# A selective-scan stack on one core: decay factors in four SBUF buffers, a four-bank PSUM ring, and a new table of places

## The chip, the cores and the metric

The kernel runs on one core of one Trainium2 chip. The metric is the device time of one execution in microseconds (us). The engines are TensorE (PE in the rows), VectorE (DVE), ScalarE (ACT), GpSimd (POOL) and SyncE (SP), which issues the DMAs. PEld is TensorE's weight load.

## The reference

A layer norm of x (4 sequences of 1024 tokens, 256 wide) feeds two branches: eight selective-scan layers, and a routed feed-forward with eight experts. The result is x + s * silu(f). The diff touches the layers alone. One of them computes:

```python
xz = jnp.einsum('bld,ed->ble', x, Wi)
xin, z = jnp.split(xz, 2, axis=-1)
xin = _silu(_causal_conv(xin, cw, cb))
x_dbl = jnp.einsum('blc,ec->ble', xin, Wx)
delta = jax.nn.softplus(jnp.einsum('blr,cr->blc', dt_raw, Wdt) + bdt)
A = -jnp.exp(Alog)
# for each time step, with a state h of 512 channels x 16
h = h * jnp.exp(d_t[..., None] * A) + (d_t * u_t)[..., None] * B_t[:, None, :]
y = jnp.einsum('bcn,bn->bc', h, C_t)
# behind the scan
y = (y + u * Dp) * _silu(z)
x = x + jnp.einsum('blc,dc->bld', y, Wo)
```

## The kernel before

`program` runs `experts`, then `mamba`, then `finish`. Only `mamba` is changed.

**Units and tiles.** The work of `mamba` is cut into 64 units: 8 layers, 4 sequences, and 2 halves of 512 time steps. A unit has 16 steps, one for each state index n, and each step has 4 tiles, one for each block of 128 channels. A tile (n, j) has number k = 4n + j and is 128 channels by 512 time steps. A tile is made as follows:
- ScalarE computes the decay, exp(delta * A), in `exponent` (L907), into one of two PSUM buffers `ps_d`. It waits until the scan two tiles back has read the buffer.
- GpSimd multiplies du by the row of B, which a DMA has repeated over the partitions in `brep`, giving the drive (L875). There are eight drive buffers, so GpSimd may be eight tiles ahead of the scans.
- VectorE runs the recurrence as one scan instruction over 512 time steps in `scan` (L1069), into one of two state buffers for the step. In second halves (h = 1) it starts from `carry`, which GpSimd copies (L861) from the last column of the first half.

When a step's four scans are done, TensorE turns the state (`turn_state`, L1225; four transposes for each of four blocks of time), ScalarE multiplies by C while it copies out (`weigh`, L914, to `prod`), and TensorE turns the product back and adds it up in `ps_y` over the 16 steps (`turn_back`, L1232).

**The ring.** All other results of TensorE pass through the same ring `ps_r`, which has two banks, in a fixed order with the turned states: the count of overflows CNT, the two output projections O0 and O1 of the unit before, X0 to X3 and Z0 to Z3 (input projections), C3 (the convolution of one channel block, by matmul), XD (B, C and the time-step rank), BC (B and C turned) and DT0 to DT3. TensorE writes into a bank when what lay in it has been read (`place`, `place_free`). ScalarE reads most of the items, VectorE reads CNT, O0 and O1.

**Three units at a time.** In unit U the engines also do the early part of unit U+2 (marks, liveness, mask, X, convolution), the late part of U+1 (XD, delta, du, Z) and the end of U-1 (gates, output projection, residual add). Where each piece stands is given by tables: `RING_AT` for TensorE, and `SILU_AT`, `EXP_AT`, `LN_AT` for ScalarE, `MARK_AT`, `ALIVE_AT`, `ADD_AT`, `GATE_AT`, `SOFT_AT`, `CONV_AT`, `DU_AT` for VectorE, `HALO_AT`, `XM_AT` for GpSimd. A pair (n, j) means: behind tile j of step n. Each engine runs its list in order, and semaphores tie the lists together. ScalarE reads a ring item one place behind the one where TensorE makes it (`READ_AT`).

**The silus.** At `SILU_AT` ScalarE does the silu of xc (L942) and of z (L946), 2048 elements each, between two loads of function tables (L942, L1020).

**Marks and liveness.** VectorE marks values over a limit (L1078, L1080, to `over`), TensorE counts them, and a running minimum (L1091, to `alive`, one buffer for each half) gives a mask. GpSimd multiplies the input by it (L846, to `xm`), and a DMA stores its first row.

**Other names in the rows.** `xc` is the convolution, with a first tap (L1104) and further taps (L1108) on VectorE for three channel blocks; `low`, `soft`, `relu` and `delta` are the steps of softplus (L1127, L1130, L1134, L1137); `du` is delta * u (L1117); the gates are L1167 and the residual add is L1173.

Of the kernel before, what the change touches and what calls it, by code (L numbers as in the profile page):

```python
# [25 lines left out]
F32 = mybir.dt.float32  # L26
# [45 lines left out]
XD = RANK + 2 * STATES  # L72
BREP = 4
DRIVE = 8
CARRY_LAG = 9
TABLE = "natural_log_exp_and_others"


RING_AT = {"CNT": (3, 0), "O0": (4, 1), "O1": (5, 3), "XD": (4, 2), "BC": (7, 3), "DT0": (6, 0), "DT1": (6, 2), "DT2": (8, 0),
           "DT3": (9, 2), "Z0": (10, 1), "Z1": (11, 3), "Z2": (14, 1), "Z3": (15, 0), "X0": (5, 0), "X1": (8, 3),  # L80
           "X2": (10, 3), "X3": (14, 2), "C3": (17, 0)}
SILU_AT, EXP_AT, LN_AT = (4, 2), [(7, 0), (10, 1)], [(8, 3), (11, 3)]
MARK_AT, ALIVE_AT, ADD_AT = [(2, 1), (2, 2)], (3, 1), [(4, 3), (6, 1)]
PE_CONV, DVE_CONV = [3], [0, 1, 2]
GATE_AT, SKIPY_AT = [(1, 1), (1, 2), (1, 2), (1, 2)], [(1, 1), (1, 3), (1, 3), (1, 3)]
SOFT_AT = [(7, 3), (8, 3), (9, 3), (10, 2), (10, 3), (11, 3), (14, 2), (14, 3)]
CONV_AT = [(5, 2), (5, 2), (6, 0), (6, 2), (9, 2), (10, 1), (12, 2), (12, 3), (15, 1), (17, 0), (17, 3), (19, 0)]
DU_AT = [(14, 3), (14, 3)]
HALO_AT, XM_AT = (3, 2), (5, 1)
CONV_ITEMS = [f"C{j}" for j in PE_CONV]  # L90
CV = CB - len(PE_CONV)
READ_AT = {name: divmod(CB * n + t + 1, CB) for name, (n, t) in RING_AT.items()}
# [509 lines left out]
def item_place(U, h, kind, name):  # L602

    i = ITEMS[kind].index(name)
    if isinstance(items_before(U, kind)[0], int):
        return (items_before(U, kind)[0] + i) % 2
    return (h * len(ITEMS["mid"]) + PRE_ALL + i) % 2


def item_ready(U, kind, name):  # L610
# [22 lines left out]

def place_free(U, kind, name):

    i = ITEMS[kind].index(name)
    if kind == "pre0" and i < 2:
        return None
    act, vec = reads(U, kind, i - 1)
    if i >= 2 and ITEMS[kind][i - 2] in VEC_ITEMS:  # L640
        return "vec", vec
    return "act", act


def mamba(nc, w_in, w_x, w_dt, w_out, w_skip, w_conv, a_log, par, xres, ident, alive_dram, bc_dram, rate_dram):

    with ExitStack() as ctx:
# [13 lines left out]
        ones_time = sb("ones_time", [1, T], BF16)  # L661
        zeros = sb("zeros", [P, 1])

        over = sb("over_mark", [P, 2, DB, T], BF16)
        alive = [sb(f"alive{h}", [P, T]) for h in range(2)]
        xm = [sb(f"xm{h}", [P, DB, T]) for h in range(2)]
        low = sb("low", [P, 2, T])
        xpad = sb("xpad", [P, CB, TAPS - 1 + T])
# [12 lines left out]

        brep = sb("brep", [P, BREP, T])
        drive = sb("drive", [P, DRIVE, T])
        state = [sb(f"state{k}", [P, CB, T]) for k in range(2)]
        carry = sb("carry", [P, STATES, CB])
        prod = sb("prod", [P, TC, INNER])

        ps_d = ctx.enter_context(nc.psum_tensor("ps_d", [P, 2, T], F32))
        ps_r = ctx.enter_context(nc.psum_tensor("ps_r2", [P, 2, 512], F32))
        ps_y = ctx.enter_context(nc.psum_tensor("ps_y", [P, CB, T], F32))  # L690

        par_in, par_exp, par_set, par_out = sem("par_in"), sem("par_exp"), sem("par_set"), sem("par_out")
# [15 lines left out]
        def is_first(U):  # L708
            return isinstance(U, int) and U == 0
# [13 lines left out]
        def _(sp):  # L723
# [22 lines left out]
            def store_alive(U, kind, G):  # L746
                h = G % 2
                sp.wait_ge(ring_vec, item_read(U, kind, "CNT"))
                c = (G // HALVES % BATCH) * SEQ + h * T
                sp.dma_start(alive_dram[:, c:c + T], alive[h][0:1, :]).then_inc(alive_out[h], 16)  # L750

            def store_bc(U, kind, F):
                sp.wait_ge(ring_act, item_read(U, kind, "XD"))
# [81 lines left out]
        def _(pool):  # L835
# [5 lines left out]
            def mask_x(U, kind, G, h, it):  # L841
                pool.wait_ge(ring_vec, item_read(U, kind, "CNT"))
                if not (isinstance(G, int) and G < 2):

                    pool.wait_ge(ring_ready, items_before(U, kind)[0])
                nc.gpsimd.tensor_tensor(xm[h][:], xres[:, :, bass.ds((it % BATCH) * SEQ + h * T, T)],  # L846
                                        alive[h][:].unsqueeze(1).to_broadcast([P, DB, T]), ALU.mult).then_inc(xm_set, 1)

            def halo(U, kind, F, h):

# [45 lines left out]
        def _(act):  # L896
            def exponent(U, h, k):

                n, j = divmod(k, CB)
                if k in (0, CB // 2):  # L900
                    act.wait_ge(delta_set, 2 * U + k // 2 + 1)
                if not (is_first(U) and k < 2):
                    act.wait_ge(scanned, TILES * U + k - 1)
                a = j * STATES + n
                if k == 0:
                    act.wait_ge(cur_in[h], loads_of(U, h))
                nc.scalar.activation(ps_d[:, k % 2, :], delta[h][:, j, :], ACT.Exp, scale=cur[h][:, a:a + 1]).then_inc(decay_set, 1)  # L907
# [137 lines left out]
            exponent(0, 0, 0)  # L1045
            exponent(0, 0, 1)
# [5 lines left out]
        def _(dve):  # L1052
            def scan(U, h, it, kind, n, j):
                k = CB * n + j
                dve.wait_ge(decay_set, TILES * U + k + 1)
                dve.wait_ge(drive_set, TILES * U + k + 1)
                if j == 0 and not (is_first(U) and n < 2):

                    if n >= 2:
                        dve.wait_ge(ring_ready, item_ready(U, kind, ("S", n - 2, TC - 1)))  # L1060
                    elif n == 1:
                        dve.wait_ge(ring_ready, item_ready(U, kind, ("S", "prev", TC - 1)))
                    else:
                        dve.wait_ge(ring_ready, items_before(U, kind)[0])
                    if h == 0 and n >= 2:
                        dve.wait_ge(carried, STATES * it + n - 1)
                    if h == 1:
                        dve.wait_ge(carried, STATES * it + min(STATES - 1 + n, STATES))
                nc.vector.tensor_tensor_scan(state[n % 2][:, j, :], ps_d[:, k % 2, :], drive[:, k % DRIVE, :],  # L1069
                                             carry[:, n, j:j + 1] if h == 1 else 0.0, ALU.mult, ALU.add).then_inc(scanned, 1)  # L1070

            def mark_over(U, kind, F, h, it, side):

                if kind != "pre0":
                    dve.wait_ge(ring_vec, items_before(U, kind)[1])
                xs = xres[:, :, bass.ds((it % BATCH) * SEQ + h * T, T)]
                if side == 0:
                    nc.vector.tensor_scalar(over[:, 0], xs, LIMIT, None, ALU.is_gt).then_inc(over_set, 1)  # L1078
                else:
                    nc.vector.tensor_scalar(over[:, 1], xs, -LIMIT, None, ALU.is_lt).then_inc(over_set, 1)  # L1080

            def keep_alive(U, h, kind, F, hf):

                dve.wait_ge(ring_ready, item_ready(U, kind, "CNT"))
                if not (isinstance(F, int) and F < 2):
                    dve.wait_ge(xm_set, F - 1)
                    if isinstance(F, int):
# [444 lines left out]
```

## Time and profile before

| | |
|---|---|
| median of 3 runs | 7806.82 us (7770.17 to 7848.79) |
| profiled execution | 7796.76 us, span 7795.0 us |
| TensorE busy | 6935.7 us (89%), weight load 4781.3 us (61%) |
| VectorE busy | 6645.2 us (85%), 6512 instructions |
| ScalarE busy | 6436.9 us (83%) |
| GpSimd busy | 5919.1 us (76%) |
| DMA | 352.40 MB, 45 GB/s |

The profile is one execution. A group line gives the source line, the engine, what is written and read, the number of instructions, their busy time and mean, and the idle time of the engine in front of them with what ended it. A timeline row gives a start, a length and how many equal instructions are merged in it; it can start before the stretch asked for. The end of one instruction overlaps the start of the next on an engine by about 0.08 us. Ends of matmuls are modelled, so TensorE is better read from starts.

### The profile page before, as it was taken

Reading aid. Unit: us, or ns where it says so; the run is one execution under the profiler, and the core shown is the slowest. Engines: PE = TensorE matmul, PEld = TensorE weight load, DVE = VectorE, ACT = ScalarE, POOL = GpSimd, SP = SyncE. Lnnn points to the kernel's source line nnn. Section 1 sums busy time; section 2 is a strip of 40 time slices with the busy share of each in tenths; the row PEclk is TensorE's granted clock in tenths of the full one; section 3 lists DMA queues with packets and bytes.
Section 4 is the critical chain, followed back from the end, with each engine's and each line's share of the span. In section 5 each row is a group of like instructions: output and inputs, shape, how many; then the busy total and the mean of one; then the engine's idle time right before and its main releaser. Section 6 shows DMA issues by size and latency. Waiting matters only on the chain. (4 is left out here: it accounts for less than half of the span.)

```text
span 7795.0 us, 144019 instructions
## 1 busy us (share of the span) xinstructions
PE 6935.7 (89%) x39999; PEld 4781.3 (61%) x40063; DVE 6645.2 (85%) x6512; ACT 6436.9 (83%) x10314; POOL 5919.1 (76%) x4917
## 2 busy tenths in 40 slices
PE   6978999888999999999899999999998899999887
PEld 4646666666666666666666666666666666666665
DVE  3259888988988898889888988988898898889888
ACT  2248888888888888888888888888888888888887
POOL 2137888787888888888878887888888778888875
PEclk9989999999999999999999999999999999999998
DMA  4111111111111111111111111111111111111112
GB/s 160 33 40 37 39 40 47 42 38 38 42 45 43 39 39 43 46 40 40 39 46 44 40 38 42 45 42 39 39 47 42 38 39 42 45 43 39 39 38 90
DMA packets 222613, 352.40 MB, mean 45 GB/s; under 512 B 43856, under 2 KB 78448, under 8 KB 221712
## 3 DMA queue, kind: packets, MB, share of 16 engines
q1 hardware_dynamic: 218048, 332.70, 14.5%
q0 software_dynamic: 3792, 10.38, 0.4%
q8 instruction: 365, 5.98, 0.3%
q14 instruction: 408, 3.34, 0.1%
HBM read 325.00 MB, written 17.98 MB: 44 GB/s over the span
## 5 line engine op out<-in xcount | busy, mean ns | idle before, releaser
L875 POOL TENSOR_TENSOR drive<-du,brep 128x512 f32<-128x512 f32 x4096 | 5495.8, 1371 | 715.0 <-DVE du L1117 360.0
L907 ACT ACTIVATE ps_d<-delta,cur 128x512 f32<-128x512 f32 x4096 | 2844.6, 695 | 447.3 <-DVE state L1069 428.1
L914 ACT ACTIVATE prod<-ps_r,bcT 128x512 f32<-128x512 f32 x4096 | 2807.1, 685 | 240.0 <-PE ps_r L1225 235.4
L1225 PE MATMUL ps_r<-ident,state 128*128 128x128 f32 x16384 | 2552.5, 279 | 326.1 <-ACT prod L914 180.5
L1069 DVE TENSOR_TENSOR_SCAN state<-ps_d,carry,drive 128x512 f32<-128x512 f32 x2048 | 2503.2, 1264 | 308.9 <-PE ps_r L1225 274.8
L1069 DVE TENSOR_TENSOR_SCAN state<-ps_d,drive 128x512 f32<-128x512 f32 x2048 | 2390.7, 1207 | 300.8 <-PE ps_r L1225 239.6
L1232 PE MATMUL ps_y<-ident,prod 128*128 128x128 f32 x16384 | 2467.1, 275 | 25.9 <-ACT prod L914 25.9
L1232 PEld LDWEIGHTS ps_y<-ident,prod 128*128 128x128 f32 x16384 | 1928.7, 142 | 663.5 <-issue 511.7
L1225 PEld LDWEIGHTS ps_r<-ident,state 128*128 128x128 f32 x16384 | 1834.7, 141 | 773.4 <-ACT prod L914 497.3
L1273 PE MATMUL ps_r<-xm,w_inz_sb 128*128 128x512 f32 x1024 | 509.1, 620 | 89.3 <-ACT prod L914 89.3
L1265 PE MATMUL ps_r<-xm,w_inx_sb 128*128 128x512 f32 x1024 | 509.1, 621 | 25.4 <-ACT prod L914 13.9
L1313 PE MATMUL ps_r<-relu,w_out_sb 128*128 128x512 f32 x1024 | 474.2, 606 | 58.7 <-ACT prod L914 56.0
L1108 DVE SCALAR_TENSOR_TENSOR xc<-xpad,taps,xc 128x512 f32<-128x512 f32 x576 | 505.4, 877 | 4.2 <-issue 1.5
L861 POOL COPY carry<-state 128x4 f32<-128x4 f32 x512 | 226.3, 442 | 232.2 <-DVE state L1069 230.3
L1306 PE MATMUL ps_r<-xdbl,w_dt_sb 16*128 16x512 f32 x512 | 290.1, 647 | 90.2 <-DVE xres L1173 47.2
L1313 PEld LDWEIGHTS ps_r<-relu,w_out_sb 128*128 128x128 f32 x1024 | 184.7, 190 | 273.3 <-issue 217.7
L1273 PEld LDWEIGHTS ps_r<-xm,w_inz_sb 128*128 128x128 f32 x1024 | 174.4, 190 | 270.1 <-ACT prod L914 134.5
L1265 PEld LDWEIGHTS ps_r<-xm,w_inx_sb 128*128 128x128 f32 x1024 | 175.9, 191 | 196.0 <-issue 154.5
L534 ACT ACTIVATE hid<-ps_t,b_sb 128x128 f32<-128x128 f32 x312 | 84.8, 382 | 227.5 <-PE ps_t L495 227.5
L1292 PE MATMUL ps_r<-u,w_x_sb 128*48 128x512 f32 x512 | 233.7, 600 | 34.1 <-ACT u L942 34.1
L462 POOL DMA_INDIRECT ys_dram<-yb,row x39 | 37.4, 959 | 296.8 <-DVE yb L554 296.8
L1243 PE MATMUL ps_y<-u,skip 128*128 128x512 f32 x512 | 241.3, 594 | 4.6 <-DVE relu L1167 4.5
(148 smaller groups left out, 4586.5 us busy)
## 6 DMA issues: line engine op xcount, KB each, us to landing
brep<-bc_dram SPq DMA_DIRECT2D x1024, 256.0 KB, 3.2
w_sb<-w SPq DMA_DIRECT2D x8, 1024.0 KB
w_all<-w SPq DMA_DIRECT2D x8, 1024.0 KB, 11.4
xb<-xs_dram SPq DMA_DIRECT2D x39, 128.5 KB, 2.0
w_all<-x SPq DMA_DIRECT2D x4, 1024.0 KB, 9.0
w_inx_sb<-w_in SPq DMA_DIRECT2D x8, 512.0 KB, 4.0
w_inz_sb<-w_in SPq DMA_DIRECT2D x8, 512.0 KB, 4.4
w_out_sb<-w_out SPq DMA_DIRECT2D x8, 512.0 KB, 4.3
```

Of the source, the lines that this page charges most:

```text
L875: nc.gpsimd.tensor_tensor(drive[:, k % DRIVE, :], du[:, j, :], brep[:, n % BREP, :], ALU.mult).then_inc(drive_set, 1)
L907: nc.scalar.activation(ps_d[:, k % 2, :], delta[h][:, j, :], ACT.Exp, scale=cur[h][:, a:a + 1]).then_inc(decay_set, 1)
L914: nc.scalar.activation(prod[:, t, :], ps_r[:, item_place(U, h, kind, item), :], ACT.Copy, scale=bcT[(h + 1) % 2 if item[1] == "prev" else ...
L1069: nc.vector.tensor_tensor_scan(state[n % 2][:, j, :], ps_d[:, k % 2, :], drive[:, k % DRIVE, :], carry[:, n, j:j + 1] if h == 1 else 0.0, ...
L1108: step = nc.vector.scalar_tensor_tensor(xc[:, j, :], xpad[:, j, tap:tap + T], w, xc[:, j, :], ALU.mult, ALU.add)
L1225: last = nc.tensor.transpose(out[:, j * P:(j + 1) * P], state[n % 2][:, j, t * P:(t + 1) * P], ident[:])
L1232: last = nc.tensor.matmul(ps_y[:, j, t * P:(t + 1) * P], prod[:, t, j * P:(j + 1) * P], ident[:], start=False, stop=True, is_transpose=Tru ...
L1243: last = nc.tensor.matmul(ps_y[:, j, :], skip[:, j, :], u[:, j, :], start=True, stop=True, skip_group_check=True)
L1265: last = nc.tensor.matmul(out, w_inx_sb[:, k, j * P:(j + 1) * P], xm[h][:, k, :], start=(k == 0), stop=(k == DB - 1))
L1273: last = nc.tensor.matmul(out, w_inz_sb[:, k, j * P:(j + 1) * P], xm[hf][:, k, :], start=(k == 0), stop=(k == DB - 1))
L1306: nc.tensor.matmul(out, w_dt_sb[:, j * P:(j + 1) * P], xdbl[0:RANK, :], start=True, stop=True).then_inc(ring_ready, 1)
L1313: last = nc.tensor.matmul(out, w_out_sb[:, j, k * P:(k + 1) * P], gated[:, j, :], start=(j == 0), stop=(j == CB - 1))
```

## The change

- The decays go to four buffers `decay` in SBUF, no longer to two in PSUM. ScalarE starts four tiles ahead (`LEAD`), not two.
- The two banks that this frees go to the ring, which has four now (`RING`). `place_free` waits for the item four back, also over the border between units.
- SBUF is won for the decays: the marks lie in the second half of `soft`, and one `alive` buffer serves both halves. The marks wait until the delta of the next unit is made, and the liveness scan waits for the mask product and the DMA store of the half before.
- Every table of places is new. The silus stand at (2, 1), not at (4, 2). `LOW_AT` is added and used nowhere.

```diff
+LEAD = 4
+RING = 4
...
-SILU_AT, EXP_AT, LN_AT = (4, 2), [(7, 0), (10, 1)], [(8, 3), (11, 3)]
-MARK_AT, ALIVE_AT, ADD_AT = [(2, 1), (2, 2)], (3, 1), [(4, 3), (6, 1)]
+SILU_AT, EXP_AT, LN_AT = (2, 1), [(9, 1), (12, 3)], [(11, 2), (14, 0)]
+MARK_AT, ALIVE_AT, ADD_AT = [(1, 0), (1, 1)], (2, 2), [(2, 3), (4, 2)]
...
-HALO_AT, XM_AT = (3, 2), (5, 1)
+HALO_AT, XM_AT = (1, 3), (5, 1)
...
-    return (h * len(ITEMS["mid"]) + PRE_ALL + i) % 2
+    return (h * len(ITEMS["mid"]) + PRE_ALL + i) % RING
...
-    i = ITEMS[kind].index(name)
-    if kind == "pre0" and i < 2:
+    i = ITEMS[kind].index(name) - RING
+    if kind == "pre0" and i < 0:
         return None
-    act, vec = reads(U, kind, i - 1)
-    if i >= 2 and ITEMS[kind][i - 2] in VEC_ITEMS:
-        return "vec", vec
-    return "act", act
+    if i < 0:
+        before = {"pre1": "pre0", "first": "pre1", "mid": "mid", "near": "mid", "last": "near", "end": "last"}[kind]
+        assert not any(x in VEC_ITEMS for x in ITEMS[before][i:])
+        return "act", items_before(U, kind)[2] + i + 1
+    act, vec = reads(U, kind, i + 1)
+    return ("vec", vec) if ITEMS[kind][i] in VEC_ITEMS else ("act", act)
...
-        over = sb("over_mark", [P, 2, DB, T], BF16)
-        alive = [sb(f"alive{h}", [P, T]) for h in range(2)]
+        alive = sb("alive", [P, T])
...
+        over = soft[:, 2:4, :].rearrange("p a t -> p (a t)").bitcast(BF16).rearrange("p (s k t) -> p s k t", s=2, k=DB)
...
+        decay = sb("decay", [P, LEAD, T])
...
-        ps_d = ctx.enter_context(nc.psum_tensor("ps_d", [P, 2, T], F32))
-        ps_r = ctx.enter_context(nc.psum_tensor("ps_r2", [P, 2, 512], F32))
+        ps_r = ctx.enter_context(nc.psum_tensor("ps_r2", [P, RING, 512], F32))
...
-                if not (is_first(U) and k < 2):
-                    act.wait_ge(scanned, TILES * U + k - 1)
+                if not (is_first(U) and k < LEAD):
+                    act.wait_ge(scanned, TILES * U + k + 1 - LEAD)
...
-                nc.scalar.activation(ps_d[:, k % 2, :], delta[h][:, j, :], ACT.Exp, scale=cur[h][:, a:a + 1]).then_inc(decay_set, 1)
+                nc.scalar.activation(decay[:, k % LEAD, :], delta[h][:, j, :], ACT.Exp, scale=cur[h][:, a:a + 1]).then_inc(decay_set, 1)
...
-                        k = CB * n + t + 2
+                        k = CB * n + t + LEAD
...
-                nc.vector.tensor_tensor_scan(state[n % 2][:, j, :], ps_d[:, k % 2, :], drive[:, k % DRIVE, :],
+                nc.vector.tensor_tensor_scan(state[n % 2][:, j, :], decay[:, k % LEAD, :], drive[:, k % DRIVE, :],
...
                     dve.wait_ge(ring_vec, items_before(U, kind)[1])
+                    dve.wait_ge(delta_set, 2 if kind == "pre1" else 2 * U + 2)
...
-                if not (isinstance(F, int) and F < 2):
-                    dve.wait_ge(xm_set, F - 1)
+                if not is_first(F):
+                    dve.wait_ge(xm_set, F)
                     if isinstance(F, int):
-                        dve.wait_ge(alive_out[hf], 16 * (F // 2))
+                        dve.wait_ge(alive_out[1 - hf], 16 * ((F + hf) // 2))
```

VectorE's list from the start of unit 1, before. The gates are `relu<-ps_y,zs`, the marks `over_mark<-xres`, the residual add `xres<-xres,ps_r`; a scan is listed as SCALAR_TENSOR_TENSOR into `state`.

```order
L1069 SCALAR_TENSOR_TENSOR state<-ps_d,carry,drive 128x512
L1167 TENSOR_TENSOR relu<-ps_y,zs 128x512 x3
L1069 SCALAR_TENSOR_TENSOR state<-ps_d,carry,drive 128x512
L1108 SCALAR_TENSOR_TENSOR xc<-xpad,taps,xc 128x512
L1069 SCALAR_TENSOR_TENSOR state<-ps_d,carry,drive 128x512 x2
L1078 TENSOR_SCALAR over_mark<-xres 128x1024
L1069 SCALAR_TENSOR_TENSOR state<-ps_d,carry,drive 128x512
L1080 TENSOR_SCALAR over_mark<-xres 128x1024
L1069 SCALAR_TENSOR_TENSOR state<-ps_d,carry,drive 128x512 x2
L1108 SCALAR_TENSOR_TENSOR xc<-xpad,taps,xc 128x512
L1069 SCALAR_TENSOR_TENSOR state<-ps_d,carry,drive 128x512
L1091 SCALAR_TENSOR_TENSOR alive<-ps_r,alive,zeros 128x512
```

The same place of the changed kernel, from the first two gates on; the marks are `soft<-xres` now.

```order
L1173 TENSOR_TENSOR relu<-ps_y,zs 128x512 x2
L1114 SCALAR_TENSOR_TENSOR xc<-xpad,taps,xc 128x512
L1086 TENSOR_SCALAR soft<-xres 128x1024
L1074 SCALAR_TENSOR_TENSOR state<-decay,carry,drive 128x512
L1173 TENSOR_TENSOR relu<-ps_y,zs 128x512 x2
L1074 SCALAR_TENSOR_TENSOR state<-decay,carry,drive 128x512 x4
L1097 SCALAR_TENSOR_TENSOR alive<-ps_r,alive,zeros 128x512
L1074 SCALAR_TENSOR_TENSOR state<-decay,carry,drive 128x512
L1179 TENSOR_TENSOR xres<-xres,ps_r 128x512
```

Thirteen scans stood between the last gate and the first residual add (seven in the piece shown up to the liveness scan, six more behind it), and five stand there now. The marks come before the last gates, and the two conv taps that stood behind the gates have gone ahead.

ScalarE's list around the silus of unit 0, before.

```order
L914 ACTIVATE prod<-ps_r,bcT 128x512
L907 ACTIVATE ps_d<-delta,cur 128x512
L942 ACT_TABLE_LOAD
L942 ACTIVATE u<-xc 128x2048
L946 ACTIVATE zs<-zs 128x2048
L1020 ACT_TABLE_LOAD
L914 ACTIVATE prod<-ps_r,bcT 128x512
L907 ACTIVATE ps_d<-delta,cur 128x512
L954 ACTIVATE xdbl<-ps_r 48x512
```

The same in the changed kernel.

```order
L919 ACTIVATE prod<-ps_r,bcT 128x512
L912 ACTIVATE decay<-delta,cur 128x512
L947 ACT_TABLE_LOAD
L947 ACTIVATE u<-xc 128x2048
L951 ACTIVATE zs<-zs 128x2048
L1025 ACT_TABLE_LOAD
L919 ACTIVATE prod<-ps_r,bcT 128x512
L912 ACTIVATE decay<-delta,cur 128x512
```

Nine tiles (two steps and a tile) lie between the old place and the new. The decay in front of the table load is that of tile 20 before and of tile 13 now, and the copy of XD no longer stands right behind the silus.

## Rows read from the trace of the kernel before

**Rows 1.** Busy time by engine, 3000 to 4000 us; then TensorE's granted clock, DMA.
```profile
3000.00:4000.00 1000.00, 905.50 (x5320) 621.86 (x5328) 892.70 (x845) 875.12 (x1375) 810.83 (x661) 1.00 0.14 42
```
**Rows 2.** The scan's line: ns minimum/median/maximum, first and last start in us.
```profile
L1069 DVE TENSOR_TENSOR_SCAN state<-ps_d,drive x2048: 1189/1207/1226, 519.1 to 7640.6; 128x512 f32<-128x512 f32 x187
L1069 DVE TENSOR_TENSOR_SCAN state<-ps_d,carry,drive x2048: 1248/1259/1285, 632.0 to 7727.5; 128x512 f32<-128x512 f32 x187
```
**Rows 3.** VectorE's groups, 3000 to 4000 us: busy us, mean ns, idle before.
```profile
L1069 DVE TENSOR_TENSOR_SCAN state<-ps_d,drive 128x512 f32<-128x512 f32 x306 | 357.4, 1207 | 44.6 <-PE ps_r L1225 36.5 <-ACT ps_d L907 7.2
L1069 DVE TENSOR_TENSOR_SCAN state<-ps_d,carry,drive 128x512 f32<-128x512 f32 x262 | 320.5, 1264 | 38.0 <-PE ps_r L1225 33.8 <-ACT ps_d L907 3.9
...
L1137 DVE TENSOR_TENSOR delta<-low,relu 128x1024 f32<-128x1024 f32 x18 | 21.5, 1197 | 0.0
```
**Rows 4.** VectorE's waits, 3000 to 4000 us: total us, times, longest.
```profile
DVE state L1069 <- PE ps_r L1225: 70.3, 35, 5.2
DVE xres L1173 <- PE ps_r L1313: 18.9, 9, 2.3
```
**Rows 5.** ScalarE in order of time, 3041 to 3048 us: start, us.
```profile
3041.34 1.28 ACT L942 ACT_TABLE_LOAD   x1
...
3046.37 1.28 ACT L1020 ACT_TABLE_LOAD   x1
```
**Rows 6.** VectorE in order of time, 3043 to 3050 us; idle before in brackets.
```profile
3043.76 0.69 DVE L1173 TENSOR_TENSOR xres<-xres,ps_r 128x512 f32 x1 [2.34 <-PE ps_r L1313]
3049.45 1.22 DVE L1069 TENSOR_TENSOR_SCAN state<-ps_d,drive 128x512 f32<-128x512 f32 x1 [5.01 <-PE ps_r L1225]
```
**Rows 7.** GpSimd in order of time, from 3092 us.
```profile
3092.00 3.74 POOL L875 TENSOR_TENSOR drive<-du,brep 128x512 f32<-128x512 f32 x3
```
**Rows 8.** VectorE in order of time, the same stretch.
```profile
3091.90 3.45 DVE L1069 TENSOR_TENSOR_SCAN state<-ps_d,drive 128x512 f32<-128x512 f32 x3
```
**Rows 9.** VectorE at 3116.6 us.
```profile
3116.48 1.22 DVE L1117 TENSOR_TENSOR du<-delta,u 128x1024 f32<-128x1024 f32 x1
```
**Rows 10.** GpSimd at 3116 to 3118 us.
```profile
3116.73 2.09 POOL L875 TENSOR_TENSOR drive<-du,brep 128x512 f32<-128x512 f32 x1 [5.03 <-DVE du L1117]
```
**Rows 11.** VectorE at 3061 us.
```profile
3061.04 1.37 DVE L1108 SCALAR_TENSOR_TENSOR xc<-xpad,taps,xc 128x512 f32<-128x512 f32 x1
```
**Rows 12.** GpSimd up to 3061.9 us.
```profile
3057.68 4.17 POOL L875 TENSOR_TENSOR drive<-du,brep 128x512 f32<-128x512 f32 x3
```
**Rows 13.** VectorE at 3076 us.
```profile
3075.81 1.61 DVE L1130 TENSOR_TENSOR low<-soft,low 128x1024 f32<-128x1024 f32 x1
```
**Rows 14.** GpSimd at 3075 to 3077.5 us.
```profile
3075.07 1.27 POOL L875 TENSOR_TENSOR drive<-du,brep 128x512 f32<-128x512 f32 x1
3076.28 1.18 POOL L861 COPY carry<-state 128x4 f32<-128x4 f32 x1
```
**Rows 15.** ScalarE's groups, 3000 to 4000 us.
```profile
L907 ACT ACTIVATE ps_d<-delta,cur 128x512 f32<-128x512 f32 x566 | 392.8, 694 | 56.6 <-DVE state L1069 54.2
L914 ACT ACTIVATE prod<-ps_r,bcT 128x512 f32<-128x512 f32 x567 | 388.5, 685 | 33.8 <-PE ps_r L1225 33.1
...
L920 ACT ACTIVATE xpad<-ps_r 128x512 f32<-128x512 f32 x36 | 21.4, 593 | 4.8 <-PE ps_r L1265 4.8
```
**Rows 16.** GpSimd's mask product, 3000 to 4000 us.
```profile
L846 POOL TENSOR_TENSOR xm<-xres,alive 128x1024 f32<-128x1024 f32 x9 | 21.2, 2361 | 0.0
```
**Rows 17.** Busy time and granted clock in two stretches; the order of columns is that of rows 1.
```profile
6333.60:6337.00 3.40, 2.17 (x13) 1.36 (x13) 3.40 (x5) 2.16 (x4) 2.74 (x3) 1.00 0.31 76
6337.10:6340.50 3.40, 3.40 (x11) 1.43 (x9) 0.76 (x1) 2.72 (x5) 1.96 (x2) 0.50 0.04 15
```
**Rows 18.** TensorE in order of time, 6341 to 6345 us.
```profile
6341.40 1.06 PE L1225 MATMUL ps_r<-ident,state 128*128 128x128 f32 x4
6342.26 1.06 PE L1232 MATMUL ps_y<-ident,prod 128*128 128x128 f32 x4
...
6343.94 0.60 PE L1232 MATMUL ps_y<-ident,prod 128*128 128x128 f32 x4
6344.38 0.60 PE L1225 MATMUL ps_r<-ident,state 128*128 128x128 f32 x4
```

More of the change, by code:

```diff
@@ L74 @@
 DRIVE = 8
+LEAD = 4
+RING = 4
 CARRY_LAG = 9
 TABLE = "natural_log_exp_and_others"
-RING_AT = {"CNT": (3, 0), "O0": (4, 1), "O1": (5, 3), "XD": (4, 2), "BC": (7, 3), "DT0": (6, 0), "DT1": (6, 2), "DT2": (8, 0),
-           "DT3": (9, 2), "Z0": (10, 1), "Z1": (11, 3), "Z2": (14, 1), "Z3": (15, 0), "X0": (5, 0), "X1": (8, 3),
-           "X2": (10, 3), "X3": (14, 2), "C3": (17, 0)}
-SILU_AT, EXP_AT, LN_AT = (4, 2), [(7, 0), (10, 1)], [(8, 3), (11, 3)]
-MARK_AT, ALIVE_AT, ADD_AT = [(2, 1), (2, 2)], (3, 1), [(4, 3), (6, 1)]
-PE_CONV, DVE_CONV = [3], [0, 1, 2]
[L85 to L88, printed above, removed]
-HALO_AT, XM_AT = (3, 2), (5, 1)
+RING_AT = {"CNT": (1, 3), "O0": (2, 1), "O1": (3, 3), "XD": (6, 3), "BC": (8, 0), "DT0": (7, 2), "DT1": (8, 1), "DT2": (10, 1),
+           "DT3": (12, 1), "Z0": (12, 2), "Z1": (13, 2), "Z2": (15, 0), "Z3": (15, 1), "X0": (4, 3), "X1": (9, 0),
+           "X2": (13, 1), "X3": (14, 2), "C3": (16, 3)}
+SILU_AT, EXP_AT, LN_AT = (2, 1), [(9, 1), (12, 3)], [(11, 2), (14, 0)]
+MARK_AT, ALIVE_AT, ADD_AT = [(1, 0), (1, 1)], (2, 2), [(2, 3), (4, 2)]
+PE_CONV, DVE_CONV = [3], [0, 1, 2]
+GATE_AT, SKIPY_AT = [(1, 1), (1, 1), (1, 2), (1, 2)], [(1, 1), (1, 1), (1, 3), (1, 3)]
+LOW_AT = [(2, 2), (6, 3)]
+SOFT_AT = [(9, 3), (11, 0), (13, 1), (13, 2), (13, 3), (14, 1), (15, 0), (15, 1)]
+CONV_AT = [(5, 3), (7, 3), (9, 0), (9, 1), (9, 2), (12, 0), (12, 2), (12, 3), (15, 1), (16, 3), (17, 0), (17, 1)]
+DU_AT = [(14, 2), (15, 1)]
+HALO_AT, XM_AT = (1, 3), (5, 1)
 CONV_ITEMS = [f"C{j}" for j in PE_CONV]
@@ L605, in item_place @@
     if isinstance(items_before(U, kind)[0], int):
-        return (items_before(U, kind)[0] + i) % 2
-    return (h * len(ITEMS["mid"]) + PRE_ALL + i) % 2
+        return (items_before(U, kind)[0] + i) % RING
+    return (h * len(ITEMS["mid"]) + PRE_ALL + i) % RING
 def item_ready(U, kind, name):
@@ L749, in store_alive @@
                 c = (G // HALVES % BATCH) * SEQ + h * T
-                sp.dma_start(alive_dram[:, c:c + T], alive[h][0:1, :]).then_inc(alive_out[h], 16)
+                sp.dma_start(alive_dram[:, c:c + T], alive[0:1, :]).then_inc(alive_out[h], 16)
             def store_bc(U, kind, F):
@@ L846, in mask_x @@
                 nc.gpsimd.tensor_tensor(xm[h][:], xres[:, :, bass.ds((it % BATCH) * SEQ + h * T, T)],
-                                        alive[h][:].unsqueeze(1).to_broadcast([P, DB, T]), ALU.mult).then_inc(xm_set, 1)
+                                        alive[:].unsqueeze(1).to_broadcast([P, DB, T]), ALU.mult).then_inc(xm_set, 1)
             def halo(U, kind, F, h):
@@ L1044, in _ @@
                     early(0, 0, "pre1", 1, n, t)
-            exponent(0, 0, 0)
-            exponent(0, 0, 1)
+            for k in range(LEAD):
+                exponent(0, 0, k)
             units(act, unit)
@@ L1084, in keep_alive @@
                 dve.wait_ge(ring_ready, item_ready(U, kind, "CNT"))
-                if not (isinstance(F, int) and F < 2):
-                    dve.wait_ge(xm_set, F - 1)
+                if not is_first(F):
+                    dve.wait_ge(xm_set, F)
                     if isinstance(F, int):
-                        dve.wait_ge(alive_out[hf], 16 * (F // 2))
+                        dve.wait_ge(alive_out[1 - hf], 16 * ((F + hf) // 2))
                     else:
-                        dve.wait_ge(alive_out[hf], 8 * (F - hf))
-                nc.vector.tensor_tensor_scan(alive[hf][:], ps_r[:, item_place(U, h, kind, "CNT"), :], zeros[:, 0:1].to_broadcast([P, T]),
-                                             alive[0][:, T - 1:T] if hf == 1 else 1.0, ALU.min, ALU.max).then_inc(ring_vec, 1)
+                        dve.wait_ge(alive_out[1 - hf], 8 * (F + hf))
+                nc.vector.tensor_tensor_scan(alive[:], ps_r[:, item_place(U, h, kind, "CNT"), :], zeros[:, 0:1].to_broadcast([P, T]),
+                                             alive[:, T - 1:T] if hf == 1 else 1.0, ALU.min, ALU.max).then_inc(ring_vec, 1)
             def conv(copied, G, h, j, k):
```

## The prediction

> **What bounds the kernel now.** I start with the loop from 3000 to 4000 us by engine: TensorE 906 us busy of 1000, VectorE 893, ScalarE 875, GpSimd 811 [rows 1]. No engine is full, so the question is how the loop turns over. The summary of the scan instruction gives the loop's length: scans start at 519.1 us, and the last starts at 7727.5 us [rows 2]. The recurrence therefore takes 7210 us for 64 units, 112.7 us a unit, and 585 us of the 7795 lie outside it. The 1000 us hold 8.87 units, so a unit has 100.6 us of VectorE, 98.6 of ScalarE and 102 of TensorE. VectorE's part is mostly its 64 scans, of 1207 ns without a carried value and 1264 with one [rows 3].
>
> The waits of VectorE in the same stretch explain most of the rest: 70.3 us on transposed states and 18.9 on the output projection, for nine residual adds [rows 4], together 9.9 us a unit. One place in order of time: ScalarE starts to load a table at 3041.34, does two silus and has the old table back at 3047.65 [rows 5]. For these 6.3 us nobody empties the ring of two banks. VectorE sits idle 2.34 us before the residual add and 5.01 us before the next scan [rows 6].
>
> **Who shares what with GpSimd.** GpSimd multiplies one drive per scan. Three drives take 3.74 us [rows 7] beside three scans that take 3.45 us [rows 8]: both keep their own pace. Those scans read one tensor from PSUM and one from SBUF. Beside VectorE instructions with both tensors in SBUF the picture is another:
> - A du product runs from 3116.48 to 3117.70 [rows 9]. A drive that began at 3116.73 takes 2.09 us and ends at 3118.82 [rows 10], 1.12 us after it.
> - The other way round, a conv tap begins at 3061.04 and takes 1.37 us, to 3062.41 [rows 11]. The drives before it end at 3061.85 [rows 12]: 0.56 us earlier.
> - A softplus subtraction of 1024 elements runs from 3075.81 to 3077.42 [rows 13]. The drive in front ends at 3076.34, so it took 1.08 us after release, and the carry copy that asked at 3076.28 ends 0.04 us behind it [rows 14]. The sum of the same size takes 1.197 us when nothing is in its way [rows 3].
>
> So they take turns by whole instructions, and about 0.12 us of the start is hidden while VectorE waits.
>
> The Trainium skill, "SBUF — State Buffer", section "Who interferes with whom", says that a VectorE instruction with two SBUF inputs contends with a GpSimd instruction that reads SBUF, and that the later one blocks until the first is done. By that rule the changed scan excludes the drive, too. The rows show it of products, taps and subtractions; no row shows a scan with two SBUF tensors.
>
> **The change, part by part.**
>
> Decays in SBUF. The exponential takes 694 ns to PSUM, and copies from PSUM to SBUF take 593 (plain) to 685 ns (scaled) [rows 15]; an exponential into SBUF may differ by 0.1 us either way, and since ScalarE has room in the longer unit below I take no difference. What counts is that all 4096 scans now have two SBUF tensors. If they must take turns, a scan's turn lies between 0.56 us (the tap over the same 512 elements) and its whole 1.21 to 1.26 us. The nearest row is the scan's own, so I take that less the hidden start: 1.09 us, 1.15 with a carry, mean 1.12 us. A drive behind it takes 1.12 us, as behind the du product.
>
> What a unit needs of this shared path:
> - 64 scans x 1.12 + 64 drives x 1.12 = 143.4 us.
> - 8 products and sums of 1024 elements x 1.08 = 8.6 us; 9 further taps x 0.56 = 5.0 us.
> - 7 instructions with one SBUF input (3 first taps of 512, 2 roundings and 2 marks of 1024). Their turn lies between nothing and that of a two-input one of their size; I take half: 3 x 0.28 + 4 x 0.54 = 3.0 us.
> - GpSimd's mask product, 2.36 us [rows 16] less a start of 0.15 = 2.2 us; 16 carry copies x 0.05 = 0.8 us.
> - Sum: 163.0 us.
>
> The gates, adds and the liveness scan (about 5 us) read PSUM and lie beside drives, since GpSimd may be eight drives ahead. If they did not, they would cost these 5 us.
>
> The ring of four and the silus. They can remove at most the 9.9 us of waits. But ScalarE has 98.6 us of work in a unit that is now far longer, so nothing on the path gets shorter by it: what comes last is the shared path. When ScalarE comes to the silus it has decays in hand for three to four tiles, 6.7 to 9.0 us of VectorE, and the silus with their tables take 6.3 us. So they are hidden; with tiles of 1.2 us, 1.5 to 3 us of them would stick out. TensorE's out projection now stands behind step 1 of the state and is due two steps earlier. It needs the four gates; five scans instead of thirteen now stand between the last gate and the first add, and at 2.24 us each they leave it 11 us, against the 16 us before.
>
> Shared buffers. One buffer for the liveness makes its scan wait for the mask product and the store of the half before; the marks, now in half of soft, wait for the delta before. VectorE would stand in both with scans behind it, and GpSimd and ScalarE behind these. By their places the partners came more than half a unit earlier (mask in step 5, liveness in step 2) or seven scans (delta in step 15, marks in step 1), so both are met: no cost. The halo copy moves from step 3 to step 1 on GpSimd, with the drives queued behind it; it waits for the last conv tap, now in step 1, with two drives made in advance, so VectorE goes on. The moved instructions keep their counts, the DMAs of brep, of the B rows and of liveness with them; SP's queue keeps its order.
>
> Waits that stay. VectorE still waits for TensorE at a few places, between 0 and today's 9.9 us a unit. I take 4: the steps are longer, but TensorE's clock may fall in its longer pauses. A unit is then 167.0 us.
>
> Sum: 63 x 167 + 146 for the last unit, which prepares no other (64 x 2.24 and the carries) = 10,667 us, plus 585 outside = 11,252 us of span. The profiled execution was 2 us longer than its span, and the median of the runs shown is 10 us above that execution: 11,264, so I say 11,260 us, 44% more than now.
>
> **Rivals.**
>
> Scans are not excluded (the silus then sit after the tenth tile with three decays in hand). For it: no row shows a scan with two SBUF tensors, and it takes some 1.2 us where a tap of its size takes its turn in 0.56, so it may hold the path otherwise. Then the waits of 9.9 us shrink to the 1.5 to 3 us of the silus that stick out, a gain of some 7.5 us a unit: 7807 - 64 x 7.5 = 7330 us. It decides if drives keep 1.27 us beside the new scans. Against it: each two-SBUF kind in the trace took turns. Chance 0.11.
>
> Half exclusion. A scan might hold the path for the 0.56 us of a tap only, and let the drive in beside it for the rest: 64 x (0.56 + 1.12) + 19.6 + 4 = 131 us a unit, 64 x 131 + 585 = 8970 us. Against it: in rows 9 to 14 what held the path held it to its end. Chance 0.05.
>
> TensorE's clock. From 6333.6 to 6337.0 TensorE worked 2.17 us at 2.4 GHz; in the stretch after it 1.2 GHz was granted [rows 17]. Four transposes then take 0.86 us from start to start (6341.40 to 6342.26), and 0.44 us at full clock (6343.94 to 6344.38) [rows 18]. At half clock all through, its 102 us would be 102 x 0.86 / 0.44 = 199 us, more than 167: 64 x 199 + 585 = 13,300 us at the worst. It will do 102 us of work in 167 us, in bursts after every fourth scan, so I expect more such stretches. But at 6343.94 it had its clock back after being busy throughout, so an engine that lags is not held at 1.2 GHz; the mechanism ends itself and the 4 us stand for it. That it binds anyway, over 180 us a unit, has 0.05 (the case of the next sentences with it).
>
> The Trainium skill, "TensorE: Matmul & The Clock Gate", Part 4, adds that transposes do not count as busy in the same way as matmuls. If so, even a full engine would stay at 1.2 GHz over transposes alone, which is the 13,300 us. The transposes of 6343.94 ran at full clock, so this trace does not bear it out.
>
> **How the numbers follow.** The forecast, exclusion with TensorE hidden, has 0.79. Its unit lies between 155 us (turns of 1.07 us, as the 1.08 of a subtraction, and no waits: 64 x 2.14 + 18) and 180 us (all of today's waits and a start shown at each scan of 0.1 us): 10,500 to 12,100 us. The three rivals lie outside and have 0.21 together, so that is the range. The runs of before spread from 7770 to 7849 us, so about 1% is what can be told from no change. Faster 0.09 (the first rival, less 0.02 in which it gives its gain back), same 0.02, slower 0.89.
>
> **What would show it.** Right: mean durations of about 2.2 us for scan and drive, a unit near 167 us, ScalarE and TensorE about 60% busy, no wait behind the silus. Right in kind and wrong in size: these durations with VectorE idle between them, or half clock through the loop. Wrong: drives of 1.27 us beside scans.

## The result and the profile after

The changed kernel takes 10,844.65 us (median of 4 runs, 10,843.96 to 10,845.63) against 7799.17 us before (median of 4 runs, the three of the table above and one more): a ratio of 1.390, interval 1.382 to 1.397. The forecast was 11,260 us. The summary of the scan's line (ns minimum/median/maximum, first and last start), which answers [rows 2]:

```profile
L1074 DVE TENSOR_TENSOR_SCAN state<-decay,drive x2048: 1191/2225/3351, 519.0 to 10638.1; 128x512 f32<-128x512 f32 x187
L1074 DVE TENSOR_TENSOR_SCAN state<-decay,carry,drive x2048: 1250/2226/2730, 674.5 to 10774.2; 128x512 f32<-128x512 f32 x187
```

The median scan takes 2.23 us where it took 1.21 and 1.26. Not all scans are longer: over the units 4 to 60, 80% take more than 1.5 us, and 20% still take 1.19 to 1.35 us, so the mean is 2.04 us. From unit 4 to unit 60 a unit is 160.9 us from its first scan to the next unit's first scan (113.0 before by the same count). What lies outside the recurrence is unchanged, 587 against 585 us. Busy time by engine from 3000 to 4000 us, the columns as in [rows 1]:

```profile
3000.00:4000.00 1000.00, 729.78 (x3708) 524.77 (x3715) 998.44 (x589) 632.22 (x966) 866.85 (x461) 0.84 0.10 28
```

VectorE reads 998 us of 1000, but with 589 instructions instead of 845. Part of this busy time is blocking: the profile counts a blocked instruction as busy from its start, as the rows in order of time below show. The groups in the same stretch, as [rows 3 and 15]:

```profile
L880 POOL TENSOR_TENSOR drive<-du,brep 128x512 f32<-128x512 f32 x401 | 810.8, 2051 | 83.5 <-DVE du L1123 53.4 <-DVE state L1074 30.2
L1074 DVE TENSOR_TENSOR_SCAN state<-decay,carry,drive 128x512 f32<-128x512 f32 x206 | 416.5, 2067 | 0.9 <-PE ps_r L1231 0.9
L1074 DVE TENSOR_TENSOR_SCAN state<-decay,drive 128x512 f32<-128x512 f32 x192 | 377.8, 2009 | 0.5
...
L912 ACT ACTIVATE decay<-delta,cur 128x512 f32<-128x512 f32 x398 | 287.3, 722 | 354.8 <-DVE state L1074 353.9
```

VectorE's waits in that stretch were 106 us before (the two kinds of [rows 4] and 16 us of smaller ones). Now they are one line:

```profile
DVE state L1074 <- PE ps_r L1231: 0.9, 3, 0.3
```

So the waits that the ring and the silus caused are gone, and four scans of five are longer instead. The reason is seen in order of time. VectorE around 3090 us:

```profile
3089.88 2.23 DVE L1074 TENSOR_TENSOR_SCAN state<-decay,drive 128x512 f32<-128x512 f32 x1
```

GpSimd at the same time:

```profile
3088.83 4.34 POOL L880 TENSOR_TENSOR drive<-du,brep 128x512 f32<-128x512 f32 x2
...
3088.83 2.19 POOL L880 TENSOR_TENSOR drive<-du,brep 128x512 f32<-128x512 f32 x1
```

The first drive ends at 3091.02. The scan started 1.14 us before that and ends at 3092.11, 1.09 us after it; the next drive starts at about 3090.99 and ends at 3093.17, 1.06 us after the scan. Over 2000 to 9000 us the medians are nearly the same: a blocked scan ends 1.08 us after the drive, a blocked drive ends 1.07 us after VectorE's instruction, and a scan behind a scan starts 2.15 us after it.

The exclusion also reaches an instruction with one SBUF tensor. The first tap reads only `xpad` and a column of `taps`. It takes 1.15 us here and 0.54 us in the run without drives that follows:

```profile
L1110 DVE TENSOR_SCALAR xc<-xpad,taps 128x512 f32<-128x512 f32 x19 | 21.8, 1148 | 0.0
```

### The profile page after: what moved, and what is told of

It reads as the page before. It is cut to its first block and busy times, and to the rows that moved or that the text cites. A ratio compares the mean times of both kernels' runs of the same rounds, so it can differ in the third digit from the quotient of the medians.

```text
span 10843.9 us, 144265 instructions
## 1 busy us (share of the span) xinstructions
PE 7909.0 (73%) x39999; PEld 5682.4 (52%) x40063; DVE 10453.6 (96%) x6512; ACT 6634.7 (61%) x10314; POOL 8982.7 (83%) x4917
## 5 line engine op out<-in xcount | busy, mean ns | idle before, releaser
L880 POOL TENSOR_TENSOR drive<-du,brep 128x512 f32<-128x512 f32 x4096 | 8285.9, 2052 | 849.1 <-DVE du L1123 551.3
L912 ACT ACTIVATE decay<-delta,cur 128x512 f32<-128x512 f32 x4096 | 2957.2, 722 | 3636.7 <-DVE state L1074 3625.3
L1231 PE MATMUL ps_r<-ident,state 128*128 128x128 f32 x16384 | 2988.9, 315 | 2352.4 <-DVE state L1074 1913.7
L1074 DVE TENSOR_TENSOR_SCAN state<-decay,carry,drive 128x512 f32<-128x512 f32 x2048 | 4128.7, 2063 | 5.5 <-PE ps_r L1231 5.4
L1074 DVE TENSOR_TENSOR_SCAN state<-decay,drive 128x512 f32<-128x512 f32 x2048 | 4028.1, 2008 | 11.9 <-PE ps_r L1231 4.3
L1231 PEld LDWEIGHTS ps_r<-ident,state 128*128 128x128 f32 x16384 | 2278.7, 164 | 2643.7 <-issue 923.1
L1238 PE MATMUL ps_y<-ident,prod 128*128 128x128 f32 x16384 | 2856.9, 306 | 19.9 <-ACT prod L919 12.9
L1238 PEld LDWEIGHTS ps_y<-ident,prod 128*128 128x128 f32 x16384 | 2268.3, 161 | 815.5 <-issue 570.7
L1114 DVE SCALAR_TENSOR_TENSOR xc<-xpad,taps,xc 128x512 f32<-128x512 f32 x576 | 755.3, 1311 | 0.5
L1140 DVE TENSOR_TENSOR low<-low,delta 128x1024 f32<-128x1024 f32 x128 | 282.0, 2203 | 0.1
```

Source lines behind the costliest of these rows:

```text
L880: nc.gpsimd.tensor_tensor(drive[:, k % DRIVE, :], du[:, j, :], brep[:, n % BREP, :], ALU.mult).then_inc(drive_set, 1)
L912: nc.scalar.activation(decay[:, k % LEAD, :], delta[h][:, j, :], ACT.Exp, scale=cur[h][:, a:a + 1]).then_inc(decay_set, 1)
L1074: nc.vector.tensor_tensor_scan(state[n % 2][:, j, :], decay[:, k % LEAD, :], drive[:, k % DRIVE, :], carry[:, n, j:j + 1] if h == 1 else 0 ...
L1114: step = nc.vector.scalar_tensor_tensor(xc[:, j, :], xpad[:, j, tap:tap + T], w, xc[:, j, :], ALU.mult, ALU.add)
L1231: last = nc.tensor.transpose(out[:, j * P:(j + 1) * P], state[n % 2][:, j, t * P:(t + 1) * P], ident[:])
L1238: last = nc.tensor.matmul(ps_y[:, j, t * P:(t + 1) * P], prod[:, t, j * P:(j + 1) * P], ident[:], start=False, stop=True, is_transpose=Tru ...
```

## The experiments

The kernel before, run again beside these, had medians of 7771 to 7813 us. An experiment of which only one run was made is marked. Runs of the kernel before lay up to 1% apart, so a smaller difference of a single run says little.

**The places and the shared buffers alone.** The decays go back to two PSUM banks, and the ring back to two.

```diff
-LEAD = 4
-RING = 4
+LEAD = 2
+RING = 2
-        decay = sb("decay", [P, LEAD, T])
+        decay = ctx.enter_context(nc.psum_tensor("ps_d", [P, LEAD, T], F32))
```

> The changed kernel with its decays back in two PSUM banks and the ring back at two: what stays is the new table of places and the shared buffers. Exclusion theory: scans read one SBUF tensor again, scan and drive go back to about 1.24 and 1.3 to 1.4 us, and the time is near that of before, 7500 to 8100 us. Rival (the new places, with their waits, cost the time, and the exclusion is only part of it): over 9000 us.

Measured: 8580.76 us, ratio 1.102 (1.100 to 1.104). Scans have 1.24 us mean again, so the exclusion of the scans went. But the time lies between the two expectations: with two banks the new places cost 12.6 us a unit (125.6 against 113.0). VectorE waits for TensorE and ScalarE, and nowhere at the marks or the liveness scan, so the shared buffers are not seen in it. Its longest waits, 3000 to 4000 us:

```profile
DVE state L1074 <- PE ps_r L1231: 109.6, 67, 5.4
DVE state L1074 <- ACT ps_d L912: 45.0, 24, 3.1
```

**The SBUF decays alone.** The old table of places in the changed kernel, and:

```diff
-LEAD = 4
-RING = 4
+LEAD = 2
+RING = 2
```

> The old table of places, the ring of two and a lead of two, with the two decay buffers in SBUF (liveness and mark buffers shared, to make room). Exclusion theory: nearly the whole loss comes from this alone, scan and drive of about 2.1 us mean, a unit of 161 to 166 us, 10,850 to 11,250 us. Rival (ring and places): near 7800 us.

Measured (one run): 10,924.18 us, 162.3 us a unit, as expected; the scans' mean of 1.91 us is under the 2.1 us expected. With the old places, a ring of two and a lead of two, the decays in SBUF bring the whole loss.

**No drives**

```diff
-                        nc.gpsimd.tensor_tensor(drive[:, k % DRIVE, :], du[:, j, :], brep[:, n % BREP, :],
-                                                ALU.mult).then_inc(drive_set, 1)
+                        pool.sem_inc(drive_set, 1)
```

> The changed kernel without GpSimd's 4096 products: the drive buffers are set once to zero, and GpSimd only counts the semaphore on. The output lacks the scans' input. Exclusion theory: the scans, still reading two SBUF tensors, take 1.19 to 1.26 us, a unit is 100 to 105 us (VectorE's work and the silus' rest), 7000 to 7350 us. Rival (a scan from SBUF is slow by itself, or is slowed by ScalarE's writes of the decays): scans stay near 2 us and the time over 10,000 us.

Measured (one run): 7431.98 us, 107.55 us a unit, with scans of the same two SBUF tensors at nearly their old length (1.30 and 1.22 us against 1.26 and 1.21):

```profile
L1075 DVE TENSOR_TENSOR_SCAN state<-decay,carry,drive 128x512 f32<-128x512 f32 x309 | 387.5, 1300 | 18.6 <-PE ps_r L1232 16.3 <-ACT decay L913 2.3
L1075 DVE TENSOR_TENSOR_SCAN state<-decay,drive 128x512 f32<-128x512 f32 x288 | 339.4, 1224 | 35.0 <-PE ps_r L1232 32.0 <-ACT decay L913 2.5 <-POOLq L880 0.6
```

So a scan from SBUF is not slow by itself, and ScalarE's writes of the decays cost it at most these 3%: it is GpSimd's products that bring it to 2.2 us. The time is 1% over the range expected.

**Drives written, nothing read**

```diff
-                        nc.gpsimd.tensor_tensor(drive[:, k % DRIVE, :], du[:, j, :], brep[:, n % BREP, :],
-                                                ALU.mult).then_inc(drive_set, 1)
+                        pool.sem_inc(pool_waited, 1)
+                        nc.gpsimd.memset(drive[:, k % DRIVE, :], 0.0).then_inc(drive_set, 1)
```

> The changed kernel with each of GpSimd's products replaced by a memset of the same drive buffer: GpSimd writes as much and reads nothing. The output lacks the scans' input. If only reads of SBUF exclude each other: scans of 1.19 to 1.26 us, 7000 to 7350 us, as without the drives. If GpSimd's writes take the path too: scan and memset take turns, 64 x (1.08 + some 0.5) + 24 = 125 us a unit, about 8600 us.

Measured (one run): 7433.51 us, 107.53 us a unit, as without drives, with GpSimd writing all the while:

```profile
L881 POOL MEMSET drive<- 128x512 f32 x596 | 308.8, 535 | 408.3 <-DVE state L1074 311.0 <-DVE du L1123 97.2
```

A memset writes the same buffer as the product and reads nothing. So it is GpSimd's reading of SBUF that excludes the scan, not its writing.

**Half of each drive**

```diff
-                        nc.gpsimd.tensor_tensor(drive[:, k % DRIVE, :], du[:, j, :], brep[:, n % BREP, :],
+                        nc.gpsimd.tensor_tensor(drive[:, k % DRIVE, 0:T // 2], du[:, j, 0:T // 2], brep[:, n % BREP, 0:T // 2],
```

> The changed kernel with GpSimd multiplying 256 of each drive's 512 columns; the others stay zero. If the turns add up, GpSimd's turn falls from 1.07 to about 0.54 us and the pair from 2.15 to 1.62 us: a unit of 161 - 64 x 0.53 = 127 us, about 8700 us. If a blocked instruction pays mainly a fixed price for the hand-over, it stays over 10,000 us.

Measured (one run): 8740.35 us, 128.0 us a unit. That is 32.9 us a unit less for half the columns of 64 drives, or 0.51 us each, near half of a turn of 1.07 us. VectorE waits 3.9 us a unit for TensorE there, against 0.2 in the changed kernel; without these waits it would be 0.57 us each. A price paid mainly for the hand-over would hardly have fallen, so the price of the exclusion is mainly the length of GpSimd's turn.

**Half of the decays in PSUM**

```diff
-RING = 4
+RING = 2
...
+        def decay_at(k):
+            return ps_d[:, k % LEAD // 2, :] if k % 2 == 0 else decay_sb[:, k % LEAD // 2, :]
```

> The changed kernel with every second decay in PSUM (two banks, ring back at two) and the others in two SBUF buffers. If the cost is one turn for each scan of two SBUF tensors, half of the scans pay it: 32 x 2.15 + 32 x about 1.2 + 24 of other work is about 131 us a unit, against 124.8 with all decays in PSUM on the same ring and places: 8900 to 9400 us. If what counts is something else about the SBUF decays (any of them slows the loop as a whole), it stays near 10,800 us.

Measured (one run): 9385.62 us, 138.0 us a unit, at the top of what was expected. The two kinds of scan stand side by side in this one kernel, beside the same GpSimd:

```profile
L1079 DVE TENSOR_TENSOR_SCAN state<-decay,carry,drive 128x512 f32<-128x512 f32 x104 | 188.3, 1810 | 0.0
...
L1079 DVE TENSOR_TENSOR_SCAN state<-ps_d,carry,drive 128x512 f32<-128x512 f32 x104 | 131.7, 1267 | 32.6 <-PE ps_r L1236 32.4
```

In first halves the means are 1454 and 1209 ns. Only the scans that read their decay from SBUF are longer, by 0.54 and 0.25 us, 0.39 in the mean, and 32 of them give 12.6 us. The unit is 12.4 us longer than the 125.6 us with none in SBUF on the same places and banks. Another 22.9 us lie between this and the 160.9 us with all of them, but that kernel has four banks and fewer waits. The cost is not a clean half because not every SBUF scan finds a drive in its way: 42% of them take more than 1.5 us here, 80% in the changed kernel.

**The changed kernel on the old places**

```diff
-SILU_AT, EXP_AT, LN_AT = (2, 1), [(9, 1), (12, 3)], [(11, 2), (14, 0)]
+SILU_AT, EXP_AT, LN_AT = (4, 2), [(7, 0), (10, 1)], [(8, 3), (11, 3)]
```

(and so with each table).

> The changed kernel, four SBUF decays and ring of four, with the old table of places. Exclusion theory: the shared path sets the time and places hardly matter: 10,800 to 10,950 us, between the changed kernel (10,845) and the one with old places and two banks (10,924). Rival (the new places save VectorE's waits in the longer unit): over 11,000 us.

Measured (one run): 10,867.93 us, 161.3 us a unit. VectorE waits there, once in a unit, for up to 8.8 us:

```profile
DVE state L1073 <- PE ps_r L1230: 49.2, 6, 8.8
```

Nevertheless the unit is only 0.4 us longer, which one run doesn't tell from nothing. While VectorE stands, GpSimd goes ahead at its own pace, with four drives in 4.94 us from 3140.81 us on, that would otherwise have been in VectorE's way. 30% of the scans are not blocked here, against 20% in the changed kernel. A wait is worth its full length only where its engine sets the time alone.

**The kernel before without drives**

```diff
-                        nc.gpsimd.tensor_tensor(drive[:, k % DRIVE, :], du[:, j, :], brep[:, n % BREP, :],
-                                                ALU.mult).then_inc(drive_set, 1)
+                        pool.sem_inc(drive_set, 1)
```

> The kernel before without GpSimd's 4096 products (drive buffers once set to zero, GpSimd counts on). The output lacks the scans' input. It is the partner of the changed kernel without drives (7432 us), so the pair shows what the ring of four, the lead of four and the new places are worth without the shared path. If they do what their waits suggest (some 4 to 6 us a unit less waiting): 7650 to 7780 us. If the gain of 7432 us is only from taps and products that no longer meet drives: 7350 to 7500 us.

Measured (one run): 7687.56 us, 111.5 us a unit. Against the 107.55 us of its partner, the whole change (ring, lead, places, buffers) is worth 4.0 us a unit, 3.3% of the time, where GpSimd makes no drives. How it divides among the parts was not measured.

**Attempts at a version that beats both.** The first has the old places, two banks and the shared buffers, with the decays of tiles 21 and 22 in SBUF, made ahead of the silus, and XD later (the lines on places in these diffs are against the kernel before):

```diff
+EXTRA = [21, 22]
-"XD": (4, 2)
+"XD": (5, 1)
+            return extra[:, EXTRA.index(k), :] if k in EXTRA else ps_d[:, k % 2, :]
```

> Meant to beat both: the kernel before (decays in two PSUM banks, ring of two, old places; liveness and mark buffers shared), but the decays of tiles 21 and 22 go to two SBUF buffers and are made in front of the silus, and XD stands three places later, so that TensorE does not wait for the silu of u with a state still to be turned. If the 2.3 and 5.0 us of VectorE's waits there are from this, they shrink by some 3 to 5 us a unit, and two excluded scans cost 2 us: 7500 to 7700 us. If ScalarE's 6.3 us of silus must be paid anyway, 7750 to 7900 us.

Measured: 8414.21 us, ratio 1.078 (1.073 to 1.082). That is over both expectations. A new wait stood up, for ScalarE's copy of X0 behind the silus. It takes 7.3 us of a unit, which grew by 10 us:

```profile
DVE xc L1122 <- ACT xpad L933: 59.4, 8, 9.6
```

The two SBUF scans cost 3.0 us a unit, not 2. They take 2.74 us in the mean and up to 7.0, because GpSimd does not always give way after one instruction. Here VectorE has the second of two such scans from 3008.21 us on, and GpSimd does four drives before it; the scan ends at 3014.25, 1.08 us after them:

```profile
3005.43 8.82 DVE L1086 TENSOR_TENSOR_SCAN state<-extra,drive 128x512 f32<-128x512 f32 x2
```

```profile
3008.23 4.93 POOL L885 TENSOR_TENSOR drive<-du,brep 128x512 f32<-128x512 f32 x4
```

What decides whose turn comes next isn't settled by these runs.

Then with the taps later:

```diff
-CONV_AT = [(5, 2), (5, 2), (6, 0), (6, 2), (9, 2)
+CONV_AT = [(6, 3), (7, 1), (7, 2), (8, 1), (9, 2)
```

> As v1_extra_decays, with the four conv taps of the first channel block moved from steps 5 and 6 to steps 6 to 8, so that VectorE does not stand before ScalarE's copy of X0. In v1 that wait was 7.8 us a unit. If it goes whole: 8414 - 64 x 7.8 = about 7910 us; if the next scans' wait for turned states takes a part of it over (ScalarE's weighs come late by the silus whatever stands in front), 8000 to 8200 us. Under 7750 us it would beat the kernel before.

Measured (one run): 8521.47 us, over every expectation. The wait for X0 is gone, and others took its place and more:

```profile
DVE state L1086 <- PE ps_r L1243: 93.9, 40, 7.9
DVE state L1086 <- ACT ps_d L920: 43.7, 23, 6.6
```

And the kernel before with the two moves of places alone (XD and the taps, as in the last two diffs):

> The kernel before with only these places moved: XD three places later and the four conv taps of the first block to steps 6 to 8. No decay in SBUF. If TensorE's standing before the silu of u with a state unturned caused the 5.0 us wait, 2 to 4 us a unit are won: 7550 to 7700 us. If the wait only moves to the next step: within 1% of before.

Measured: 8101.13 us, ratio 1.043 (1.041 to 1.044): slower than either expectation. The wait of 5.0 us for turned states grew to one of up to 7.4 us in each unit. None of these three beats the kernel before. That ScalarE's 6.3 us can't be hidden with a ring of two banks is a guess from three attempts; no run shows it.

**The halo back at its place.** In the changed kernel GpSimd stands before the halo copy:

```profile
3102.72 0.33 POOL L861 MEMSET xpad<- 128x12 f32 x1 [7.41 <-DVE xc L1114]
```

and VectorE's scans meanwhile are short again, one of them here:

```profile
3099.35 1.21 DVE L1074 TENSOR_TENSOR_SCAN state<-decay,drive 128x512 f32<-128x512 f32 x1
```

```diff
-HALO_AT, XM_AT = (1, 3), (5, 1)
+HALO_AT, XM_AT = (3, 2), (5, 1)
```

> The changed kernel with the halo copy back at its old place in GpSimd's list (step 3, not step 1). In the changed kernel GpSimd stands 7.4 us before it in a unit and waits for the last conv tap, and VectorE runs its gates, marks and four scans with nobody on the other side of the path. If that is the part by which a unit (160.9 us) is longer than the turns add up to (157 us), GpSimd's drives now lie beside the gates, and a unit loses 2 to 4 us: 10,590 to 10,720 us. If the drive buffers fill up at once (GpSimd is at most eight ahead) and it stands there in place of the halo: within 0.5% of 10,845 us.

Measured: 10,818.75 us (10,817.79 to 10,820.41), 160.5 us a unit: the second outcome. GpSimd's waits, 3000 to 4000 us, have no halo any more, but more for scans (30.2 us in the changed kernel) and for the carry (7.2 us there):

```profile
POOL drive L880 <- DVE state L1074: 59.5, 48, 2.4
...
POOL carry L866 <- DVE state L1074: 21.4, 6, 4.8
```

GpSimd's waits add up to 134 us there and to 133 us in the changed kernel. The eight drive buffers fill, and GpSimd stands there instead.

## Why the prediction was right, and where its sizes were off

- **Exclusion of scan and drive: right.** It was read from products, taps and subtractions in the trace of before and carried over to an instruction that no row showed. The changed trace shows the turns. The run with memsets shows that GpSimd's reading is the cause, the run with half of the decays in PSUM that the scan's second SBUF tensor is, and the run with half the columns that the price is mainly the length of GpSimd's turn.
- **The pair of turns: 2.24 us forecast, 2.15 measured.** The drive's 1.12 us was taken from one place behind a product; it is 1.07 us (-3.2 us a unit). The scan's mean was 1.12 us, with 1.15 for those with a carried value; a blocked scan ends 1.08 us after the drive with or without one, so the start of 0.06 us for the carry is hidden, too (-2.6 us).
- **Waits that stay: 4 us forecast, 0.2 measured** (-3.8 us).
- **The sum of the turns: right as a first estimate, 4 us short.** With the measured turns it gives 64 x 2.15 + 19.6 = 157 us, and the unit is 160.9 us. A truer way to add is from VectorE, which hardly ever stands idle: without drives it is busy 924 us of 1000, 99.4 us of a unit of 107.55; with them 160.7 us. GpSimd's reads thus add 61 us, 0.96 us a drive, not the whole 1.07. Compared by kind in these two traces, 49.6 of the 61 us are in the scans, 5.3 in the further taps, 1.8 in the first taps, and 4.6 in the steps of softplus. Gates, adds, marks, the liveness scan and the du product keep their length. So the gates and adds cost the shared path nothing by themselves, as forecast, but GpSimd doesn't always use it meanwhile: it is idle 21.8 us of a unit, 2.2 us of them beside gates and marks. That the 4 us came from the wait before the halo was a guess, and the run with the halo back shows that it was not: it gave 0.4 us. The traces don't say which single term of the sum was short.
- **One SBUF tensor: half a turn was a guess.** The first taps are lengthened by 0.6 us each, the roundings by 0.26 us and the marks by nothing, 2.3 us together for a forecast of 3.0.
- **Sum.** 6.1 us a unit too much, 390 us in 64 units, is nearly all of 11,260 - 10,845. The three terms above are 9.6 us too high together and the sum is 4 us short elsewhere, so part of the closeness is luck.
- **The silus hidden, shared buffers free, code outside unchanged: right.** From 3000 to 4000 us VectorE has no wait above 0.3 us. ScalarE was busy 632 us of 1000, near the 60% forecast. The exponential took 722 ns to SBUF against 694 to PSUM, within the 0.1 us allowed for it.
- **TensorE's clock: right that it falls and does not bind.** 31% of the recurrence was granted 1.2 GHz (mean 0.84 in the stretch above). At that clock its instructions take longer, so it was busy 73% of the time, not the 60% forecast. The case of 13,300 us did not come: in the changed trace the granted clock rose to 2.4 GHz 519 times, 122 of them after 10 us in which TensorE started nothing but transposes.
- **The rival without exclusion** was priced at 7330 us; with GpSimd's products taken out the same program runs in 7432 us. Half exclusion fell: 8970 us was forecast for it, and 10,845 was measured.

## What to carry to other kernels

Before an operand is moved from PSUM to SBUF, count the SBUF tensors that each VectorE instruction will read, and look for GpSimd instructions that read SBUF beside it. In the trace of before, the test is to find any VectorE instruction with two SBUF tensors and to compare the GpSimd instruction beside it with its usual length: here 2.09 us against 1.27. An instruction with one SBUF tensor needs the same test, since the scan with one was free and the first tap was not. A VectorE that reads 998 us busy of 1000 may be blocked for over a third of it; the sign is a longer mean of the same form. Where two engines take turns, add up turns, not busy shares; a wait of one of them then costs little. Here two such waits, of 7.4 and 8.2 us a unit, were worth 0.4 us each.

## What the runs showed that was not expected

- A blocked scan of 512 elements ends 1.08 us after the drive, as late as a sum or subtraction of 1024 elements does and twice as late as a further tap of 512 (0.55 us). It holds the path to its end: a drive that waits for it ends 1.07 us behind it.
- A memset on GpSimd (0.54 us for 128x512) ran beside such scans without costing them anything: 7433.5 against 7432.0 us, one run each.
- The new places cost 10% with two banks: 8581 us. With four banks and no drives, the kernel that has them is 4.0 us a unit better than the old one. A table of places is tuned to its ring.
- Turns need not alternate: one scan stood behind four drives in a row and took 6.04 us.
